# A graph and attention kernel: own orders for the first and the last two steps, TensorE warmed, the last group's x added on the chip, copy and load paced, PV ahead of V

## The reference

```python
# x: 128 x 128 x 256 (batch, node, feature), adj: 128 x 128
h = relu(layernorm(x))
# layer 0, W1 = W2 = adj, nodes mixed:
A = adj @ h ; C = adj @ h + b
out0 = max over features of relu(A[:, :, None, :] + (C - A)[:, :, :, None])
x = x + out0
h = relu(layernorm(x))
# layer 1, 8 heads of 32:
q, k, v = split(h @ w_qkv)
attn = softmax(where(adj == 0, -inf, q @ k.T * 32 ** -0.5))
o = (attn @ v) @ w_proj + b_proj
x = x + o + layernorm(o) * gamma + beta
```

## Time and profile before

| what | value |
|---|---|
| median of 3 runs | 781.08 us (778.01 to 782.69) |
| the profiled execution | 781.43 us |
| its span, first to last instruction | 779.7 us |
| busy: PE, DVE, ACT, POOL | 724.6, 606.4, 466.1, 395.3 us |
| granted clock of TensorE, mean | 0.983 |
| DMA | 71.0 MB, mean 91 GB/s |

### The profile page before, as it was taken

The page is one execution under the profiler, slowest core; times in us unless marked ns, Lnnn a source line. Parts: engine busy times, 40 slices in busy tenths (PEclk is TensorE's granted clock), DMA queues, the critical chain, the costliest instruction groups (busy, mean ns, idle before and its releaser), DMA issues.

```text
span 779.7 us, 37319 instructions
## 1 busy us (share of the span) xinstructions
PE 724.6 (93%) x16233; PEld 490.2 (63%) x16233; DVE 606.4 (78%) x1458; ACT 466.1 (60%) x1033; POOL 395.3 (51%) x720
## 2 busy tenths in 40 slices
PE   1789999999999999999999999999999999999851
PEld 0356666666666666666666666666666766666540
DVE  3568888787888888888888888888888888878642
ACT  4456675556666655667666556676665566774420
POOL 4324455554556455554564554545545546454433
PEclk9999999999999999999999999999999999999975
DMA  6333335535544665464455544543455345424222
GB/s 191 104 84 84 59 83 110 111 87 108 70 86 96 112 110 96 99 112 77 77 98 110 111 93 102 111 70 81 102 111 111 87 108 110 84 38 77 29 28 28
DMA packets 102835, 71.01 MB, mean 91 GB/s; under 512 B 68369, under 2 KB 101905, under 8 KB 102161
## 3 DMA queue, kind: packets, MB, share of 16 engines
q1 hardware_dynamic: 85776, 51.85, 26.9%
q0 software_dynamic: 16896, 16.78, 16.7%
...
## 4 chain that ended last, share of the span: by engine, by line
PE 90%; DVE 3%; ACT 2%; issue 2%; DMA 1%; POOL 1%; SPq 0%; DVEq 0%; POOLq 0%
PE a_ps L309 21%; PE sum_ps L427 11%; PE a_ps L321 11%; PE pv_ps L396 8%; PE sum_ps L399 7%; PE sc_ps L375 6%; PE sc_ps L350 6%; PE sc_ps L330 6%; PE a_ps L291 5%; PE sum_ps L424 3%; PE pv_ps L411 2%; PE sc_ps L379 2%; PE sc_ps L356 1%; DVE smax L649 1%; DMA w_sb<-in_L_gnn_w_qkv 1%
## 5 line engine op out<-in xcount | busy, mean ns | idle before, releaser
L542 ACT ACTIVATE p_sb<-sc_ps 128x512 f32<-128x512 f32 x256 | 140.4, 607 | 37.2 <-PE sc_ps L379 37.2
L649 DVE TENSOR_REDUCE smax<-sc_ps 128x4 f32<-128x512 f32 x256 | 157.6, 677 | 1.8 <-PE sc_ps L350 1.8
L834 POOL TENSOR_TENSOR oT_lo<-oT,oT_hi 128x256 f16<-128x256 f32 x128 | 83.4, 672 | 132.1 <-ACT oT_hi L555 132.1
L309 PE MATMUL a_ps<-hT,w_hi 128*128 128x512 f16 x512 | 133.2, 383 | 5.9 <-DMA hT<-h_parts 3.2
L548 ACT ACTIVATE pv_sb<-pv_ps 128x512 f32<-128x512 f32 x64 | 38.2, 597 | 144.6 <-PE sum_ps L399 144.6
L637 DVE TENSOR_TENSOR qk_lo<-a_ps,qk_hi 128x512 f16<-128x512 f32 x128 | 87.4, 683 | 29.7 <-ACT qk_hi L529 29.5
L396 PE MATMUL pv_ps<-p_sb,v_sb 128*32 128x128 f32 x2048 | 104.9, 276 | 1.9 <-ACT pv_sb L548 1.3
L399 PE MATMUL sum_ps<-p_sb,sel_sum 128*32 128x128 f32 x2048 | 103.4, 273 | 0.0
L687 DVE BATCH_NORM_STATS2 st<-o_sb 128x6 f32<-128x256 f32 x128 | 53.6, 420 | 49.5 <-ACT o_sb L561 49.4
L828 POOL TENSOR_TENSOR h_parts<-h_sb,h_parts 128x256 f16<-128x256 f32 x128 | 82.1, 673 | 18.8 <-ACT h_parts L507 18.7
L529 ACT ACTIVATE qk_hi<-a_ps 128x512 f16<-128x512 f32 x128 | 77.4, 604 | 9.4 <-PE a_ps L309 9.3
...
## 6 DMA issues: line engine op xcount, KB each, us to landing
x_sb<-in_x SPq DMA_DIRECT2D x32, 512.0 KB, 5.4
out<-in_x SPq DMA_DIRECT2D x32, 512.0 KB, 5.5
out<-y_sb POOLq DMA_DIRECT2D x32, 512.0 KB, 6.2
...
hT<-h_parts SPq DMA_TRANSPOSE x33, 4.6
...
```

What stands on the lines that cost most here:

```text
L309: mm = nc.tensor.matmul(a_ps[c % 2][:].rearrange("p (b n) -> p b n", b=G), w[:, dc, col:col + P], hT[:, par, part, :, dc], start=(k == 0), ...
L542: nc.scalar.activation(p_sb[:, j, i], sc_ps[i][:], ACT.Exp, scale=SCALE).then_inc(p_ready, 1)
L649: nc.vector.tensor_reduce(smax[:, i, 0, j], sc_ps[i][:], AX.X, ALU.max).then_inc(smax_ready, 1)
L834: nc.gpsimd.tensor_tensor(oT_lo[:, b], oT[:, b], oT_hi[:, b], ALU.subtract).then_inc(olo_ready, 1)
```

## The change

- `pipeline` takes three lists: `first` for step 0, `order` for steps 1 to 31, and `last` for what is left of groups 30 and 31. In `last` an item with "+" belongs to group 31's last part, so both groups are interleaved freely.
- All five steady orders are changed. PE: V0 goes ahead of K1, V1 behind P3; R1 ahead of K0; O0, L0, O1 in place of O0, Q3, O1, L0. ACT, DVE and POOL follow.
- PE does the mask constants ahead of everything else and then AWAKE = 26 matmuls of 512 columns of the identity into sc_ps[3], whose result nothing reads; only then it waits for w_hi and w_lo. w_hi is made by DVE instead of ACT. Waits for constants move from the begins of steps to where they are used.
- For the last two groups `o_ps` alternates between the upper halves of a_ps[0] and a_ps[1], with a wait for the copy two before instead of one before.
- The last group isn't copied from x to out; POOL adds beta to x_sb (`add_beta`), `finish` adds this in place of beta, and SP stores it in two halves without accumulation (`store_last`).
- `copy_x` also waits for the row maxima's transpose of the step before, `load_x` also for the first scores of its step, and SP's order is C0 X0 T0.

```diff
-        o_ps = sum_ps[:, 2:4].rearrange("p c n -> p (c n)")
+        def o_ps(g, b):
+            return a_ps[b % 2][:, D:] if g >= STEPS - 2 else sum_ps[:, 2:4].rearrange("p c n -> p (c n)")
...
-        def pipeline(step):
-            for t in range(STEPS + 2):
-                step(t, t % SLOTS, t < STEPS, 1 <= t <= STEPS, t >= 2, t + 1 < STEPS, t + 2 < STEPS, t + 3 < STEPS)
+        def pipeline(step, first, order, last):
+            for t in range(STEPS):
+                for what in (first if t == 0 else order):
+                    step(t, what[0], int(what[1]), *phases(t))
+            for what in last:
+                t = STEPS + len(what) - 2
+                step(t, what[0], int(what[1]), *phases(t))
...
             def copy_x(t):
                 wait(sp, copied, 16 * t)
+                wait(sp, maxT_psum, t)
...
+            def store_last(i):
+                sp.wait_ge(y_ready, G * (STEPS - 1) + 2 * (i + 1))
+                half = slice(2 * i, 2 * i + 2)
+                nc.sync.dma_start(og[STEPS - 1][:, half], y_sb[:, half]).then_inc(last_stored, 16)
...
                 wait(sp, h_ready, G * (t - 2))
+                wait(sp, s_psum, DC * (t - 3) + 1)
...
+                if t == 1:
+                    sp.wait_ge(qk_psum, 1)
...
-            ORDER = ("C0 T0 X0").split()
+            ORDER = ("C0 X0 T0").split()
+            FIRST = ("T0 X0 C0").split()
+            LAST = ("D0+ D1+").split()
...
+            pe.wait_ge(pool_const, 2)
             pe.wait_ge(act_const, 2)
-            pe.wait_ge(dve_const, 3)
+            pe.wait_ge(dve_const, 4)
...
+            for _ in range(AWAKE):
+                nc.tensor.matmul(sc_ps[3][:], identb[:], identb[:].unsqueeze(1).to_broadcast([P, HC, P]),
+                                 start=True, stop=True)
+            pe.wait_ge(dve_const, 6)
...
-                    wait(pe, o_ready, G * g)
+                    wait(pe, o_ready, G * min(g, STEPS - 2))
...
-                wait(pe, o_ready, G * g + b)
+                if g < STEPS - 2:
+                    wait(pe, o_ready, G * g + b)
+                else:
+                    pe.wait_ge(v_ready, 2 * STEPS)
+                    pe.wait_ge(o_ready, G * g + b - 1)
...
-            ORDER = ("Q0 Y0 Y1 Y2 Y3 N0 E0 Q1 R0 Q2 K0 S0 R1 O0 Q3 O1 L0 N1 E1 O2 L1 O3 K1 S1 V0 V1 P0 P1 P2 P3 M0").split()
+            ORDER = ("Q0 Y0 Y1 Y2 Y3 N0 E0 Q1 R0 Q2 R1 K0 S0 Q3 O0 L0 O1 N1 E1 O2 L1 O3 V0 K1 S1 P0 P1 P2 P3 V1 "
+                  "M0").split()
+            FIRST = ("Q0 Q1 Q2 K0 S0 Q3 L0 L1 K1 S1 V0 V1 M0").split()
+            LAST = ("Y0 Y1 Y2 N0 Y3 E0 R0 N1 E1 R1 O0 O1 P0 P1 P2 P3 O2 O3 Y0+ Y1+ Y2+ Y3+ R0+ R1+ O0+ O1+ O2+ "
+                  "O3+").split()
...
-            ORDER = ("Y0 Q0 E0 E1 E2 Q1 E3 C0 Q2 R0 R1 R2 O0 C1 R3 H0 Q3 H1 H2 H3 O1 E4 E5 O2 E6 E7 O3 V0 L0 A0 M0 V1").split()
+            ORDER = ("Q0 Y0 R0 E0 E1 E2 Q1 E3 C0 Q2 H0 C1 R1 H1 R2 O0 R3 H2 H3 O1 Q3 E4 O2 E5 E6 E7 O3 A0 V0 M0 "
+                  "V1 L0").split()
+            FIRST = ("R0 H0 R1 R2 R3 H1 H2 H3 Q0 Q1 Q2 Q3 Z0 Z1 V0 L0 V1 M0").split()
+            LAST = ("Y0 E0 E1 E2 E3 C0 E4 E5 E6 E7 C1 O0 O1 A0 O2 O3 Y0+ C0+ C1+ O0+ O1+ O2+ O3+").split()
...
-            ORDER = ("I0 I1 Q0 I2 O0 Q1 Q2 O1 S0 S1 S2 S3 Q3 B0 X0 B1 B2 L0 B3 L1 G0 S4 S5 S6 S7 F0 U0 F1 F2 F3 X1 M0").split()
+            ORDER = ("I0 I1 Q0 I2 O0 Q1 O1 Q2 S0 S1 S2 S3 L0 B0 Q3 X0 B1 B2 B3 X1 G0 L1 S4 S5 S6 S7 U0 F0 M0 F1 "
+                  "F2 F3").split()
+            FIRST = ("X0 X1 Q0 Q1 Z0 Q2 S0 S1 S2 Q3 S3 L0 L1 S4 S5 S6 S7 U0 M0 Z1").split()
+            LAST = ("I0 I1 I2 O0 O1 B0 B1 B2 B3 G0 I0+ I1+ I2+ O0+ F0 O1+ F1 F2 F3 B0+ B1+ B2+ B3+ G0+ F0+ F1+ "
+                  "F2+ F3+").split()
...
+                        if g == STEPS - 1:
+                            dve.wait_ge(xb_ready, b + 1)
+                        rest = x_sb[:, g % SLOTS, b] if g == STEPS - 1 else beta_sb[:]
...
+                nc.vector.tensor_scalar(w_hi[:], w_sb[:], WS, 0.0, ALU.mult, ALU.add).then_inc(dve_const, 1)
...
+            def add_beta(g, b):
+                if b == 0:
+                    pool.wait_ge(h_ready, G * (g + 1))
+                nc.gpsimd.tensor_tensor(x_sb[:, g % SLOTS, b], x_sb[:, g % SLOTS, b], beta_sb[:], ALU.add).then_inc(
+                    xb_ready, 1)
...
-            ORDER = ("C0 C1 C2 C3 H0 H1 H2 H3 N0 W0 W1 W2 K0 W3 D0 X0").split()
+            ORDER = ("C0 C1 H0 C2 H1 H2 H3 C3 N0 W0 W1 K0 W2 W3 X0 D0").split()
+            FIRST = ("Z0 H0 X0 H1 H2 H3").split()
+            LAST = ("C0 C1 B0+ C2 C3 N0 W0 W1 W2 W3 B1+ C0+ C1+ C2+ C3+ D0 K0 B2+ N0+ W0+ W1+ W2+ W3+ B3+").split()
```

More of the change, by code:

```diff
@@ L476, in _, with step @@
-            pipeline(step)
+            ORDER = ("Q0 Y0 Y1 Y2 Y3 N0 E0 Q1 R0 Q2 R1 K0 S0 Q3 O0 L0 O1 N1 E1 O2 L1 O3 V0 K1 S1 P0 P1 P2 P3 V1 "
[3 more added lines that the diff above has]
+                  "O3+").split()
+            def step(t, kind, i, k, a, e, d, prep, norm, load):
+                if kind == "L" and a:
+                    layer0(t, k, i)
+                elif kind == "Q" and a:
+                    project_qk(t, k, i)
+                elif kind == "V" and a:
+                    project_v(t, k, i)
+                elif kind == "K" and a:
+                    mask_scores(t, i, e)
+                elif kind == "S" and a:
+                    scores(t, i)
+                elif kind == "M" and a:
+                    transpose_max(t)
+                elif kind == "N" and e:
+                    mask_scores_T(t - 1, i, a)
+                elif kind == "E" and e:
+                    scores_T(t - 1, i)
+                elif kind == "P" and e:
+                    values(t - 1, (k + 2) % SLOTS, i)
+                elif kind == "Y" and d:
+                    values(t - 2, (k + 1) % SLOTS, PAIR + i)
+                elif kind == "R" and d:
+                    spread(t - 2, i)
+                elif kind == "O" and d:
+                    project_o(t - 2, i)
@@ L479, in _ @@
+            pipeline(step, FIRST, ORDER, LAST)
         @block.scalar
@@ new lines, in _, with step @@
+            FIRST = ("R0 H0 R1 R2 R3 H1 H2 H3 Q0 Q1 Q2 Q3 Z0 Z1 V0 L0 V1 M0").split()
+            LAST = ("Y0 E0 E1 E2 E3 C0 E4 E5 E6 E7 C1 O0 O1 A0 O2 O3 Y0+ C0+ C1+ O0+ O1+ O2+ O3+").split()
+            def step(t, kind, i, k, a, e, d, prep, norm, load):
+                if kind == "L" and a:
+                    layer0_numbers(t, k)
+                elif kind == "Q" and a:
+                    qk_high(t, i)
+                elif kind == "V" and a:
+                    take_v(t, k, i)
+                elif kind == "M" and a:
+                    max_high(t)
+                elif kind == "E" and e:
+                    exps(t - 1, i)
+                elif kind == "A" and e:
+                    take_pv(t - 1, 0)
+                elif kind == "Y" and d:
+                    take_pv(t - 2, 1)
+                elif kind == "O" and d:
+                    take_o(t - 2, i)
+                elif kind == "C" and d:
+                    o_high(t - 2, i)
+                elif kind == "R" and prep:
+                    rectify(t + 1, (k + 1) % SLOTS, i)
+                elif kind == "H" and prep:
+                    h_high(t + 1, (k + 1) % SLOTS, i)
+                elif kind == "Z" and i == 0:
@@ L596, in _ @@
             act.wait_ge(adjT_ps, 1)
             nc.scalar.activation(adjT_hi[:], sc_ps[0][:, 0, :], ACT.Copy, scale=WS).then_inc(act_const, 1)
-            act.wait_ge(core_load, 16)
-            nc.scalar.activation(w_hi[:], w_sb[:], ACT.Copy, scale=WS).then_inc(act_const, 1)
+            mask_constants()
             for b in range(G):
                 rectify(0, 0, b)
-            for b in range(G):
-                h_high(0, 0, b)
-            mask_constants()
+                if b > 0:
+                    h_high(0, 0, b - 1)
@@ L605, in _ @@
+            h_high(0, 0, G - 1)
             take_masks()
-            act.wait_ge(c_load, 16 * 5)
-            pipeline(step)
+            pipeline(step, FIRST, ORDER, LAST)
         @block.vector
@@ L716, in step @@
-            def step(t, k, a, e, d, prep, norm, load):
-                if t == 0:
+            ORDER = ("I0 I1 Q0 I2 O0 Q1 O1 Q2 S0 S1 S2 S3 L0 B0 Q3 X0 B1 B2 B3 X1 G0 L1 S4 S5 S6 S7 U0 F0 M0 F1 "
[3 more added lines that the diff above has]
+                  "F2+ F3+").split()
+            def step(t, kind, i, k, a, e, d, prep, norm, load):
+                if kind == "I" and d:
+                    invert_sums(t - 2, i)
+                elif kind == "O" and d:
+                    scale_o(t - 2, i)
+                elif kind == "B" and d:
+                    stats_o(t - 2, i)
+                elif kind == "G" and d:
+                    aggregate_o(t - 2)
+                elif kind == "F" and d:
+                    finish(t - 2, i)
+                elif kind == "S" and a:
+                    row_max(t, i)
+                elif kind == "U" and a:
+                    repeat_max(t)
```

(12 more changed lines are left out.)

215 lines of the change are left out of this document (71 added, 144 removed).

## The result

The changed kernel takes 754.69 us (median of 4 runs, 754.19 to 756.43) against 781.14 us of the kernel before on the same chip: a ratio of 0.9676, 95% interval 0.9648 to 0.9703. The profiled execution took 754.41 us for a span of 752.5 us. The forecast was 754.3 us and 752.6 us of span.

What follows compares the result with a forecast made beforehand. Steps were taken as bound by TensorE, both ends by chains round all engines. Start 32.35, step 1 18.35, steps 2 to 31 664.2 and drain 37.7 sum to 752.6 us of span; with 1.7 around it, 754.3 us, range 745 to 769.

Steps and rivals of the forecast that it cites:

- The steady order: Steps 2 to 31: new engine orders shorten a step by 0.33 us to 21.99, 9.9 us over 30 steps, bounds 0 and 12.
- the tiling: Each steady step: one change of TensorE's array tiling fewer, ten left of eleven, worth 0.11 us a step.
- the wait for E7: Each steady step: K1's wait for the last exp, 0.02 us, goes since V's first matmuls now cover it.
- L1 to O3: Each steady step: O3's wait for the copy of O2 goes by copying ahead of E5, 0.20 us a step.
- thin covers of DVE's list: Steady steps: margins of 0.1 to 0.5 us before TensorE or ScalarE waits; losing one costs 0.1 to 0.3 a step.
- rival A: Steady steps don't get shorter, since TensorE waits for DVE's list or for ACT; 764 us, chance 0.2.
- Stalls: Extra time, nearly all in the first six of steps 2 to 31: 4.5 us kept, from 0 to 1.54 in every step.
- Rival B: Steps 2 to 31: no instruction-fetch stalls, the 4.5 us go; 750 us, chance 0.08.
- Start: Up to step 1: hT lands at 15.9, Q2 starts at 22.0, M0 at 32.2; step 1 starts at 32.35 instead of 36.67.
- Drain: Last two groups interleaved, last group stored in two plain halves landing in 4.2 us: 37.7 instead of 50.04 us.
- C: Steps 2 to 31: spread transfers stall each step as the worst one, 41.7 us more; 796 us, chance 0.04.
- D: Both ends: the clock doesn't rise in the warming (+2.9 us) or the drain's interleaving locks for 3 us; 760 us, chance 0.1.

Runs made afterwards that it cites:

- e5: The changed kernel without the 26 warming matmuls (AWAKE = 0); 754.09 us, ratio 0.9659 to the kernel before.
- e1: The changed kernel with the steady orders of TensorE, ScalarE, VectorE and GpSimd as before the change; 770.67 us, ratio 0.9873 to the kernel before.
- e3: The changed kernel with ScalarE's E5 put back ahead of the copy O2; 757.96 us, ratio 0.9709 to the kernel before.
- e6: The changed kernel with 34 warming matmuls instead of 26; 754.99 us, ratio 0.9673 to the kernel before.
- e7: The changed kernel with an own buffer for the last group's y, without the wait for the store; 756.41 us, ratio 0.9692 to the kernel before.
- e4: The changed kernel with copy and load unpaced (both added waits out, SP's order C0 T0 X0); 759.12 us, ratio 0.9731 to the kernel before.
- e9: The changed kernel with step 0's copies of Q0 and Q1 made earlier (on ScalarE ahead of H1 to H3) and 34 warming matmuls; 754.06 us, ratio 0.9662.
- e10: e9 with the last group's beta added earlier and an own buffer for its y; 753.38 us, ratio 0.9653 to the kernel before.

## Why the prediction was right, step by step

**The steady order: right in kind, 3 us too much.** The gain is 0.23, not 0.33 a step, 6.9 instead of 9.9 us. By distances between blocks in a quiet step: O3 to what follows 0.76 instead of 0.89, and M0 to Q0 0.11 instead of 0.16, so the tiling and the wait for E7 gave 0.18 (forecast 0.13). L1 to O3 takes 0.73 instead of 0.85: 0.12 (forecast 0.20). The 0.08 at O1 goes off again, which leaves 0.22 to 0.23. The step that failed is "the copy can start about then and end with L1: 0.20": it starts then and ends 0.08 after it, and the same 0.08 is new at O1, whose cover the new order took away; I hadn't looked at O1. None of the thin covers of DVE's list was lost (rival A): the 22.09 are all busy on TensorE, and DVE had 18.06 of work.

**V0: hardly priced.** The sum put the wait for E7 at 0.02, "now under V0". Without V0 it is 0.5 as soon as O2's copy goes ahead of E5, which is part of this same change. The sum wasn't hurt, since both came together, but whoever leaves V0 behind loses: 785.27 us.

**Stalls: wrong by 2.35 us the other way.** I kept 4.5 and found 2.15. Rival B ("the copy no longer stands in the store's way") had a part of it: unpaced, they are 6.3. The other part is chance of the layout: the same steps stalled, 2 to 7, at another place in the step, and the old orders in the same program stall in 24 to 29. The forecast kept the 4.5 without a reason beyond "no row says which steps then stall". It is luck that with the 3 us of the steady order this error cancels to 0.7.

**Start: the right end by wrong terms.** hT was to land at 15.9; TensorE started on it at 16.96. Rows of TensorE, GpSimd, DVE and SP:

```profile
7.62 7.06 PE L319 MATMUL sc_ps<-identb 128*128 128x512 bf16 x26
16.96 1.81 PE L346 MATMUL a_ps<-hT,w_hi 128*128 128x512 f16 x4 [2.27 <-DMA hT<-h_parts]
...
9.62 2.16 POOL L871 TENSOR_TENSOR h_parts<-h_sb,h_parts 128x256 f16<-128x256 f32 x1 [1.51 <-ACT h_parts L541]
9.49 1.76 DVE L805 SCALAR_TENSOR_TENSOR w_lo<-w_sb,w_hi 128x1536 f16<-128x1536 f32 x1
...
11.47 3.47 SPq L270 DMA_TRANSPOSE hT<-h_parts  x2
```

The first low part took 2.16 us, not 0.64: it started 0.13 after DVE's w_lo and didn't end before that had (9.49 + 1.76); the other three took 0.63 each, until 13.67 instead of 12.45. I had called w_lo hidden since it ends early enough itself; what GpSimd loses beside it I hadn't priced. (No run takes w_lo away; that the one slows the other is read from these rows.) The warming ended at 14.7, TensorE idled 2.27 us, and Q0 ran at the 1.2 GHz level again (1.81 for four, as in the earlier trace rows). So the warming bought nothing (without it M0 comes at the same 32.08, e5), and there was little for it to buy: Q2 wants the copies, which ScalarE makes behind H1 to H3. There the forecast held: Q2 at 21.81 (22.0), M0 at 32.08 (32.2). The late hT and the cold clock were both hidden behind ScalarE's list. Even where Q0 and Q1 ran fast (unpaced: Q0's four in 1.02), M0 came at 32.19.

One thing was not foreseen: in four kernels' profiles (e1, e3, e6, e7) M0 comes at 34.0 to 34.5. Their rows are alike; of e7, TensorE and ScalarE:

```profile
16.86 1.02 PE L347 MATMUL a_ps<-hT,w_hi 128*128 128x512 f16 x4 [1.05 <-DMA hT<-h_parts]
...
22.38 1.45 PE L347 MATMUL a_ps<-hT,w_hi 128*128 128x512 f16 x4 [2.77 <-DVE qk_lo L674]
...
24.71 0.60 ACT L566 ACTIVATE qk_hi<-a_ps 128x512 f16<-128x512 f32 x1 [2.73 <-PE a_ps L347]
```

x of group 1 lands 0.6 us later (13.9 instead of 13.3), and TensorE, warm, is through with Q0 and Q1 early, idles 2.77 and meets Q2 and S0 at the low clock, so Q2's copy comes at 24.71 instead of 23.30. In these profiles warmth won where nobody waits is lost where somebody does. It isn't a rule: in e4, e9 and e10 Q0 ran fast too and the clock stayed up.

**Drain: 37.17 for 37.7, by two errors.** The interleaving did what was forecast. Two rows of the kernel before, whose last M0 was at 729.49, and the same two blocks of the changed one (last M0 at 715.11), the first half of PV of group 31 and the last output projection:

```profile
745.54 0.43 PE L396 MATMUL pv_ps<-p_sb,v_sb 128*32 128x128 f32 x8 [0.57 <-ACT o_sb L561]
...
763.49 0.27 PE L424 MATMUL sum_ps<-bp_rows,bias_ones 128*128 128x256 f16 x1 [0.57 <-ACT o_sb L561]
```
```profile
725.34 0.43 PE L438 MATMUL pv_ps<-p_sb,v_sb 128*32 128x128 f32 x8 [0.56 <-issue]
...
740.68 0.27 PE L470 MATMUL a_ps<-bp_rows,bias_ones 128*128 128x256 f16 x1
```

16.1 us behind M0 before and 10.2 now, then 34.0 and 25.6: PV no longer stands behind the copy of O3, and 8.4 us are won by the last projection. By T, the forecast has PV at 9.75 (9.9 measured), the next group's first output projection at 20.0 (20.3) and the norm's begin ended at 28.8 (29.2).

Two terms behind it were wrong. I had y of group 31 end at T = 33.4, hence 748.7, and a 256 KB store land 4.2 later. The y wait for the store of group 30, since both use one buffer; the chain of waits and the DMA row:

```profile
740.20 6.39 DMA out<-y_sb
...
747.83 0.47 DVE y_sb L748
```
```profile
out<-y_sb SPq DMA_DIRECT2D x2, 256.0 KB, 2.2
```

The y ended 749.9, 1.2 late. The wait has only 0.3 to 0.4 of this (746.59 to 746.89 is idle). Another 0.3 is the two y beside GpSimd's beta, 1.41 us instead of 1.09, which the forecast had put at 0 ("in gaps, 0"), and 0.4 to 0.5 was there before, at the end of the norm's begin. The store landed in 2.2 us, under the lower bound of 3.3 that I had from a 64 KB load: a load's landing at the full start bounded nothing for a store into a quiet end. -2.0 and +1.2 and some 0.3 of rest make the -0.5. The missed wait is one that the code shows: `finish` waits for `stored` ahead of the first y. The large error is the store's landing.

**Rivals.** A didn't come; B in part; C not at the size feared, though stalls of its size exist: with V0 put back seven late steps take 23.7 to 24.4. D's clock half came true (Q0 ran cold) at no cost.
